# A grouped convolution with per-patch experts on one core: ScalarE's turn in another order, with the window write on its queue

## The reference, cut to what matters

```
x: (32 images, 32 channels, 32, 32), float32
v = (x - mean) / sqrt(var + 1e-5)          # over each channel's 32x32 (group norm, one channel a group)
v is padded to 40x40; patches of 8x8 with a border of 1: 5x5 per image, each 10x10, 32 channels
logits = mean of the patch @ Wg + bg        # 8 experts
routing = the largest logit's expert, with its softmax probability
y = relu(conv3x3(patch, Wexp[expert]) + bexp[expert]) * probability
out = x + y                                 # the inner 4x4 patches of each image
```

## Time and profile before

| | |
|---|---|
| time, median of 3 runs (lowest to highest) | 201.89 us (200.23 to 203.51) |
| the profiled execution: time, span | 200.15 us, 198.0 us |
| granted clock of TensorE, mean over the span | 0.829 |
| busy: PE, DVE, ACT, POOL | 107.9, 116.4, 92.9, 75.9 us |
| DMA queue 1, queue 10 | 48.8%, 28.3% of 16 engines' span |

### The profile page before, as it was taken

The page is one execution under the profiler, slowest core; times in us unless marked ns, Lnnn a source line. Parts: engine busy times, 40 slices in busy tenths (PEclk is TensorE's granted clock), DMA queues, the critical chain, the costliest instruction groups (busy, mean ns, idle before and its releaser), DMA issues.

```text
span 198.0 us, 11471 instructions
## 1 busy us (share of the span) xinstructions
PE 107.9 (54%) x4894; PEld 102.5 (52%) x4894; DVE 116.4 (59%) x270; ACT 92.9 (47%) x253; POOL 75.9 (38%) x236
## 2 busy tenths in 40 slices
PE   0004136738395709970593719960692749808930
PEld 0003135728395709960592718960692749708930
DVE  3796923625199706992199705992199309691264
ACT  2586375920693337550693237650693262513200
POOL 0850673733202671054702562043803562538000
PEclk9999999696969685698599675698599678966997
DMA  5974899776869975899559975899559956898302
GB/s 186 480 325 165 183 279 359 296 188 230 219 240 313 335 262 203 323 282 362 187 214 320 336 247 203 309 286 359 211 216 309 318 187 269 228 322 308 119 0 106
DMA packets 41553, 50.93 MB, mean 257 GB/s; under 512 B 31136, under 2 KB 33312, under 8 KB 40480
## 3 DMA queue, kind: packets, MB, share of 16 engines
q1 hardware_dynamic: 33088, 29.18, 48.8%
q10 hardware_dynamic: 8448, 21.56, 28.3%
HBM read 17.32 MB, written 14.43 MB: 160 GB/s over the span
## 4 chain that ended last, share of the span: by engine, by line
ACTq 21%; DMA 20%; DVE 16%; ACT 13%; PE 12%; SPq 8%; issue 8%; DVEq 0%
ACTq L120 13%; DMA XG<-windows 12%; PE conv_bank L507 10%; SPq L171 8%; DMA XG<-XG 6%; ACTq L437 6%; ACT WS L427 5%; ACT WIND L416 5%; DVE BLK L329 3%; DMA XT<-x 2%; ACT XN L405 2%; DVE BLK L333 2%; DVE XT L337 1%; DVE STATS L257 1%; PE pick_bank L495 1%
## 5 line engine op out<-in xcount | busy, mean ns | idle before, releaser
L507 PE MATMUL conv_bank<-XG,WS 128*32 128x64 f32 x4800 | 95.9, 253 | 42.4 <-DMA XG<-XG 35.3
L507 PEld LDWEIGHTS conv_bank<-XG,WS 128*32 128x32 f32 x4800 | 90.7, 132 | 44.6 <-DMA XG<-XG 36.9
L214 POOL COPY WS<-WP 128x192 f32 x200 | 61.9, 357 | 101.0 <-issue 64.8
L427 ACT COPY WS<-WP 128x192 f32 x200 | 54.5, 348 | 76.2 <-issue 60.2
L322 DVE STREAM_TRANSPOSE YT<-conv_bank 128x320 f32<-128x320 f32 x40 | 18.8, 493 | 18.1 <-PE conv_bank L507 18.1
L264 DVE TENSOR_SCALAR NEWT<-ROOT,VAR 128x1 f32<-128x1 f32 x8 | 2.2, 272 | 41.5 <-ACT ROOT L397 41.5
L489 PE MATMUL logit_bank<-GATE,CONST 128*100 128x8 f32 x40 | 6.1, 261 | 33.1 <-DVE GATE L287 33.1
L489 PEld LDWEIGHTS logit_bank<-GATE,CONST 128*100 128x100 f32 x40 | 5.2, 199 | 34.5 <-DVE GATE L287 18.6
L416 ACT COPY WIND<-XN 128x2500 f32<-128x2500 f32 x8 | 19.0, 2376 | 0.2
L329 DVE STREAM_TRANSPOSE BLK<-YT 128x1024 f32<-128x1024 f32 x8 | 17.9, 2231 | 1.1
L405 ACT ACTIVATE XN<-XT,NEGMR,RSTD 128x1024 f32<-128x1024 f32 x8 | 10.2, 1274 | 8.5 <-DVE NEGMR L269 8.5
(11 more groups left out here) (36 smaller groups left out, 45.9 us busy)
## 6 DMA issues: line engine op xcount, KB each, us to landing
XG<-XG ACTq DMA_DIRECT2D x30, 490.0 KB, 4.1
windows<-WIND SPq DMA_DIRECT2D x8, 1250.0 KB, 5.6
XG<-windows SPq DMA_DIRECT2D x60, 125.0 KB, 4.2
XT<-x SPq DMA_DIRECT2D x8, 512.0 KB, 6.6
out<-XT SPq DMA_DIRECT2D x16, 256.0 KB, 4.2
XG<-XG ACTq DMA_DIRECT2D x16, 240.0 KB, 2.4
XG<-windows SPq DMA_DIRECT2D x32, 62.5 KB
XG<-ones ACTq DMA_DIRECT2D x1, 1250.0 KB, 11.1
```

What stands on the lines that cost most here:

```text
L214: last = nc.gpsimd.tensor_copy(WS[:, at % RING, ACT_PAIRS + i, :], WP[:, bass.ds(index[i], PAIR)])
L427: last = nc.scalar.copy(WS[:, at % RING, i, :], WP[:, bass.ds(index[i], PAIR)])
L507: last = nc.tensor.matmul(o, WS[:, lot, n % LOT * 2 + b // 2, column:column + C], taps, start=kx == 0, stop=kx == TAPS - 1)
```

## The change

- `windows_dram` has three buffers instead of two (`WB`).
- `write_windows` moves from SyncE's list to ScalarE's, behind `windows`, for every group; ScalarE waits for the copy into WIND before it asks. `shift` is the same code at another place, called with the engine.
- ScalarE's turn begins with `copies(g,4)`, then `exponent(g+1)`, `shift(g,2)`, `normalise(g+2)`, `windows(g+2)`, `write_windows(g+2)`, then as before; `root(g+3)` stands at the turn's end instead of `root(g+2)` at its start, and `root(2)` ahead of the loop.
- VectorE: `statistics(g+3)` between lots 1 and 2 instead of `statistics(g+2)` at the turn's start; `finish` is split into `weigh` (transpose, relu and probability) and `add`, with `selection(g+1)` between them; `gate(g+2)` after lot 0's transpose instead of lot 1's.

```diff
--- before.py
+++ after.py
@@ -20,6 +20,7 @@
 LOT, LOTS = NB, NP // NB
 NCB = LOTS
 XB = 5
+WB = 3
 SQ = 32
 HALF = H * W // 2
 SEG = 2
@@ -88,7 +89,7 @@
         conv_bank = [bank(f"conv_bank{i}") for i in range(NCB)]
         logit_bank, pick_bank = bank("logit_bank"), bank("pick_bank")
 
-        windows_dram = [nc.dram_tensor(f"windows{u}", (GI * C * NP, WIN * WIN), fp32).ap() for u in range(2)]
+        windows_dram = [nc.dram_tensor(f"windows{u}", (GI * C * NP, WIN * WIN), fp32).ap() for u in range(WB)]
 
         x_loaded = [sem(f"x_loaded{i}") for i in range(XB)]
         table_loaded, small_loaded, ones_loaded = sem("table_loaded"), sem("small_loaded"), sem("ones_loaded")
@@ -131,6 +132,15 @@
                     engine.dma_start(rows, source[:, 0:PART[1] * LOT, ky * WIN:ky * WIN + TAP]
                                      ).then_inc(lower_loaded[0] if tail else first_loaded, 16)
 
+        def shift(engine, g, part):
+            first, last = PART[part] * LOT, PART[part + 1] * LOT
+            size = (last - first) * PATCH - (TAPS - 1) * WIN
+            engine.wait_ge(upper_loaded[part], UPPERS * (g if part == 0 else g + 1))
+            for ky in range(1, TAPS):
+                rows = bass.AP(XG, ky * KEPT + first * PATCH, [[ROWS * KEPT, C], [NP * PATCH, GI], [1, size]])
+                source = bass.AP(XG, first * PATCH + ky * WIN, [[ROWS * KEPT, C], [NP * PATCH, GI], [1, size]])
+                engine.dma_start(rows, source).then_inc(lower_loaded[part], 16)
+
         def lay_even(e):
             return (bass.AP(WP, e * E * PAIR, [[E * E * PAIR, KP], [PAIR, E], [1, NW]]),
                     bass.AP(BLK, e * NW, [[H * W, KP], [0, E], [1, NW]]))
@@ -147,19 +157,6 @@
             def load_x(g):
                 sp.dma_start(XT[g % XB][:], x_rows[g]).then_inc(x_loaded[g % XB], 16)
 
-            def write_windows(g):
-                sp.wait_ge(windows_ready, g + 1)
-                if g > 1:
-                    for part in range(1, SPLITS):
-                        sp.wait_ge(upper_loaded[part], UPPERS * (g - 1))
-                    if g > 2:
-                        sp.wait_ge(upper_loaded[0], UPPERS * (g - 2))
-                    else:
-                        sp.wait_ge(first_loaded, FIRSTS)
-                        sp.wait_ge(lower_loaded[0], LOWERS)
-                sp.dma_start(windows_dram[g % 2].rearrange("(p k) w -> p (k w)", k=NP), WIND[:]
-                             ).then_inc(windows_written, 16)
-
             def read_upper(g, part):
                 first, last = PART[part] * LOT, PART[part + 1] * LOT
                 sp.wait_ge(windows_written, 16 * (g + 1))
@@ -167,7 +164,7 @@
                     sp.wait_ge(conv_done, LOTS * (g - 1) + PART[part + 1])
                 for b in range(GI):
                     rows = bass.AP(XG, (b * NP + first) * PATCH, [[ROWS * KEPT, C], [PATCH, last - first], [1, PATCH]])
-                    source = windows_dram[g % 2].rearrange("(b n j) w -> b j n w", b=GI, j=C)[b]
+                    source = windows_dram[g % WB].rearrange("(b n j) w -> b j n w", b=GI, j=C)[b]
                     sp.dma_start(rows, source[:, first:last]).then_inc(upper_loaded[part], 16)
 
             def stores(g):
@@ -180,14 +177,10 @@
             load_x(1)
             load_x(2)
             load_x(3)
-            write_windows(0)
             read_first(sp, range(TAPS - 1))
             read_upper(0, 1)
             read_upper(0, 2)
-            write_windows(1)
             for g in range(GROUPS):
-                if g + 2 < GROUPS:
-                    write_windows(g + 2)
                 if g > 0 and g + 3 < GROUPS:
                     if g + 3 >= XB:
                         sp.wait_ge(out_stored, 32 * (g + 3 - XB + 1))
@@ -322,7 +315,7 @@
                 nc.vector.transpose(to, conv_bank[at % NCB][:, 0:LOT * PIX].rearrange("p (n s q) -> p n s q", s=2, q=SQ)
                                     ).then_inc(bank_free[lot], 1)
 
-            def finish(g):
+            def weigh(g):
                 for lot in range(LOTS):
                     dve.wait_ge(bank_free[lot], g + 2)
                 blocks = bass.AP(YT, 0, [[2 * NP * C, 128], [NB, KEEP], [1, KEEP], [NP * C, 2], [NP, C]])
@@ -331,6 +324,8 @@
                 patches = BLK[:].rearrange("p (k w) -> p k w", w=PIX)
                 prob = bass.AP(PBM[g % 3], 0, [[SPREAD, 128], [1, SPREAD], [0, PIX]])
                 then_next(nc.vector.scalar_tensor_tensor(patches, patches, 0.0, prob, ALU.max, ALU.mult))
+
+            def add(g):
                 for v in range(KEEP):
                     rows = XT[g % XB][:, v * PS * W:(v + 1) * PS * W].rearrange("p (i h w) -> p h i w", i=PS, h=KEEP)
                     strip = BLK[:, v * PS * W:(v + 1) * PS * W].rearrange("p (h i w) -> p h i w", i=PS, h=KEEP)
@@ -359,10 +354,9 @@
             probability(0)
             selection(0)
             gate(1)
+            statistics(2)
 
             for g in range(GROUPS):
-                if g + 2 < GROUPS:
-                    statistics(g + 2)
                 if g + 1 < GROUPS:
                     routing(g + 1)
                 if g + 2 < GROUPS:
@@ -373,19 +367,24 @@
                     nc.vector.memset(SPARE[:, LOTS:LOTS + 1], 0.0).then_inc(pick_ready, 1)
                 if g > 0:
                     turn_lot(g - 1, LOTS - 1)
-                    finish(g - 1)
+                    weigh(g - 1)
                 if g + 1 < GROUPS:
                     selection(g + 1)
+                if g > 0:
+                    add(g - 1)
                 turn_lot(g, 0)
-                turn_lot(g, 1)
                 if g + 2 < GROUPS:
                     gate(g + 2)
                 else:
                     nc.vector.memset(SPARE[:, LOTS + GROUPS - g:LOTS + GROUPS - g + 1], 0.0).then_inc(gate_ready, 1)
+                turn_lot(g, 1)
+                if g + 3 < GROUPS:
+                    statistics(g + 3)
                 turn_lot(g, 2)
                 turn_lot(g, 3)
             turn_lot(GROUPS - 1, LOTS - 1)
-            finish(GROUPS - 1)
+            weigh(GROUPS - 1)
+            add(GROUPS - 1)
 
 
         @block.scalar
@@ -427,14 +426,18 @@
                     last = nc.scalar.copy(WS[:, at % RING, i, :], WP[:, bass.ds(index[i], PAIR)])
                 last.then_inc(act_copied[lot], 1)
 
-            def shift(g, part):
-                first, last = PART[part] * LOT, PART[part + 1] * LOT
-                size = (last - first) * PATCH - (TAPS - 1) * WIN
-                act.wait_ge(upper_loaded[part], UPPERS * (g if part == 0 else g + 1))
-                for ky in range(1, TAPS):
-                    rows = bass.AP(XG, ky * KEPT + first * PATCH, [[ROWS * KEPT, C], [NP * PATCH, GI], [1, size]])
-                    source = bass.AP(XG, first * PATCH + ky * WIN, [[ROWS * KEPT, C], [NP * PATCH, GI], [1, size]])
-                    act.dma_start(rows, source).then_inc(lower_loaded[part], 16)
+            def write_windows(g):
+                act.wait_ge(windows_ready, g + 1)
+                if g >= WB:
+                    for part in range(1, SPLITS):
+                        act.wait_ge(upper_loaded[part], UPPERS * (g - WB + 1))
+                    if g > WB:
+                        act.wait_ge(upper_loaded[0], UPPERS * (g - WB))
+                    else:
+                        act.wait_ge(first_loaded, FIRSTS)
+                        act.wait_ge(lower_loaded[0], LOWERS)
+                act.dma_start(windows_dram[g % WB].rearrange("(p k) w -> p (k w)", k=NP), WIND[:]
+                              ).then_inc(windows_written, 16)
 
             act.dma_start(WT, wtab).then_inc(table_loaded, 16)
             act.dma_start(CONST[:], consts).then_inc(small_loaded, 16)
@@ -448,6 +451,7 @@
             act.wait_ge(pads_set, 1)
             normalise(0)
             windows(0)
+            write_windows(0)
             for e in ACT_LAYS[2:]:
                 last = nc.scalar.copy(*lay_odd(e))
             last.then_inc(pairs_laid, 1)
@@ -455,31 +459,34 @@
             normalise(1)
             exponent(0)
             windows(1)
+            write_windows(1)
             act.wait_ge(pairs_laid, 3)
             act.wait_ge(index_ready, 1)
             copies(0, 0)
             read_first(act, [TAPS - 1])
             for lot in range(1, LOTS - 1):
                 copies(0, lot)
-            shift(0, 1)
+            shift(act, 0, 1)
+            root(2)
             for g in range(GROUPS):
-                if g + 2 < GROUPS:
-                    root(g + 2)
+                copies(g, LOTS - 1)
                 if g + 1 < GROUPS:
                     exponent(g + 1)
+                shift(act, g, 2)
                 if g + 2 < GROUPS:
                     normalise(g + 2)
                     windows(g + 2)
-                shift(g, 2)
-                copies(g, LOTS - 1)
+                    write_windows(g + 2)
                 if g + 1 < GROUPS:
                     act.wait_ge(index_ready, g + 2)
```

(8 more changed lines are left out.)

## The result

The changed kernel takes 216.43 us (215.35 to 217.03, 4 runs) against 201.48 in the same comparison: ratio 1.076, 95% interval 1.068 to 1.083, slower. The forecast was 212.0, with 200 to 220 around it. Medians are over all executions of a kernel, ratios and their intervals over the faster ones alone, those within 1.5% of its fastest. The profiled execution took 216.41 us, its span is 214.6 against 198.0: 16.6 us to account for.

What follows compares the result with a forecast made beforehand. Bound taken: a ring of ScalarE's turn through WIND and the DMA queue. Four turns 4.2, last turn with a write 2.5, turn without one 2.2 and start 3.0 add 11.9 to 200.15: 212.0 us, range 200 to 220.

Steps and rivals of the forecast that it cites:

- The ring through ScalarE, WIND and the queue: Pace of the kernel before: ScalarE's turn to WIND, 13.32 us, then 9.1 us of SyncE's DMA queue until part 0's reads land.
- Lot 4's copies make normalise 2.9 us later: ScalarE's turn: index load 1.9, copies 1.4, exponent 0.3 and requests 0.3 put normalise at 79.8 instead of 76.87.
- The sum for a full turn: A turn with window write and x load gets 1.05 us longer: 2.96 later, 1.9 quicker.
- Root ran ahead of the turn: ScalarE: deviation is long done when normalise comes, so the 1.03 us from root to normalise goes.
- The write's alternation with the reads: DMA queues: 1.4 small read packets pass per large write packet, about 180 of 1280, gaining the reads 0.3 us.
- That the reads cannot be ahead, and the write sets their landing: Part 0's reads, first requested at 82.5 to 84.2, stay behind the write's packets from 84.4; landing 90.7 against 89.66.
- TensorE isn't in it: Kernel before: part 0's first read request, after TensorE's convolutions, went at 82.09 while the queue was busy to 87.
- The turn without a write: The turn from 155.05 to 172.57: paced by exponent, index and copies; exponent 3.6 us later, index 1.43 sooner, +2.2 us.
- The start: Until the first part's request at 45.06: early write delays the root 1.6 us; request at 48.1, +3.0, bounds 0 and 4.8.
- The rest at nothing: Three DRAM buffers, selection before the adds, statistics within the turn and the earlier gate were costed at nothing.
- the load comes back at once: Rival, 13%: the index load before lot 4's copies takes 0.54 us and part 2's requests hide wholly; 200.6 us, no change.
- The reads get ahead of the write: Rival, 11%: lot 1 ends two or three microseconds before the write is asked for, ScalarE alone sets the pace; 193 us.

## Why the prediction was right, step by step

- **The ring through ScalarE, WIND and the queue: right, and shown** by the run with lot 4's copies early and the exponent ahead of them: 8.98 us from the write's request to the tap copies', and a turn of 24.9.
- **Lot 4's copies make normalise 2.9 us later: right in kind, 2.4 us by the trace.** It starts 12.0 us after the turn's first request, where it was 9.6. 2.95 from the root's end to normalise against 1.03 is 1.9, and the root itself stands 0.4 later in the turn; the write is asked for 15.7 us after the turn's first request, where it was 13.35. The forecast was 16.3: the load took 1.2 and not 1.9 in this turn, 1.6 in the middle ones. The sum for a full turn was 1.05; the middle ones took 1.2, in part by luck, as the point on the reads says.
- **"Root ran ahead of the turn": wrong in its reason.** The root at the end of a turn is the instruction right ahead of the next turn's first, so it isn't earlier at all. Its round trip through VectorE is hidden only because lot 4's copies now stand between it and normalise; in the version with these put back, normalise waits 0.83 us for VectorE again. The 1.03 was taken off rightly.
- **The write's alternation with the reads: right in kind.** 109 small packets beside 135 large ones in 3.9 us, 0.8 for each large one, with the reads asked for as it began; 1.4 was assumed. The Trainium skill's page "DMA: Bandwidth & Descriptors", section "Queues, rings and completion order", has the engines go round robin between queues by packets of typically 9 to 17 descriptors; these rows fit a grain of about one large row against one small instead.
- **That the reads cannot be ahead, and the write sets their landing: the step that was half the truth.** The times were right (lot 1's end and the write's packets within half a microsecond of each other, as the two ways in the text had it), but I took the exponent's way for a reason why the reads come late, and not as a ring of its own. It is one, of 11.4 us to the exponent and 11.9 from there to the next request, and where there is a write it was the longer by about a microsecond: that much a turn lost when the exponent came early. In all the time fell by 12 us then, more than my theory could give. The middle turns of that run are 0.5 us longer than before, and what sets them is the way through WIND; so that the changed kernel's came out at 1.2 beside a forecast of 1.05 is luck, since the ring that was summed is not the one that set them. The text also said "TensorE isn't in it" of the kernel before. The ring through tap copies, lot 0 and lot 1 reached SyncE's reads there at 82.02, and alone these need 5.3 us to the request (94.65 to 99.93 in the run with the late exponent): 20.1 against the turn's 22.4, so the statement held, by 2.3 us.
- **The turn without a write: mis-sized by 2.5 of 4.73 us, by that same omission.** I took exponent, index and copies for its ring. The exponent came 3.1 us later in the turn (11.1 against 8.0), for 3.6 forecast. But then the reads bind, as the chain shows:

```profile
178.74 0.10 ACT LEXP L409
...
180.38 3.26 PE conv_bank L514 x115
...
185.66 4.00 DMA XG<-windows
```

Lot 1 ran at a granted clock of 0.50, the lower level of 1.2 GHz, after lot 0 at 0.50 and a stand for the picks from 176.8 to 179.1; before, TensorE went from lot 0 (0.54) to the picks without a stand, and lot 1 ran at 1.00, the upper level of 2.4 GHz. The windows view, the changed kernel's row and the one of the kernel before:

```profile
179.90:183.60 3.70, 3.70 (x138) 3.69 (x141) 3.63 (x5) 0.00 (x0) 0.00 (x0) 0.50 0.10 40
```

```profile
164.80:166.80 2.00, 2.00 (x136) 1.99 (x139) 1.97 (x2) 0.13 (x1) 0.00 (x0) 1.00 0.96 375
```

The difference, 1.7 us, would be the greater part of the 2.5, an estimate from these two rows. In the run with the exponent one place earlier TensorE didn't stand there either, the clock from 172 to 176 was 1.00, and the turn took 16.34.

- **The start: right, in its two terms too.** The early write made the first convolution 2.6 us later and the root 1.1 (it began at 32.57 to 32.71 in four traces with the write on ScalarE's queue, at 31.45 to 31.49 in three with it on SyncE's), where 1.6 was taken; the new order added 1.3 to 1.7, where the sum had 1.4.
- **The first turn, +3.20 for +1.05: not foreseen.** Part 1's tap copies came 8.07 us into the turn, as they waited for late reads, against 6.95 before, and the load behind them took 2.70 us. That the x load, now freed from the write and asked for at 55.99, moved its packets in front of these copies' fits the trace; no run separated it. With group 1's write asked for later these copies came 7.25 us into the turn, and it took 24.4.
- **The rest at nothing: right**, 0.997 for all of it, the overlooked move of the logits included. The parts weren't run one by one.
- Of the rivals, "the load comes back at once" named the right lever, since the load ahead of the bulk gave 8.4 us back; but in the changed kernel it stood behind the bulk in every turn. "The reads get ahead of the write" is what the run with the exponent one place earlier shows; it paid less than the rival's 193, since the load behind the write then took 4.36 us and not the 0.55 to 1.2 that the rival wanted.

## What to carry to other kernels

Before moving work in an engine's list, follow every result that the displaced instructions make, and time each ring that closes through them from its own start to the next turn's; a ring with 3 us of slack doesn't show in the chain of waits and is next when the move is 3 us long. Two rings that both pass the point of the move have to be relieved together, and a run that relieves one tells only the distance to the other. When a change bundles a cheap gain with a dear reordering, cut it in four corners: here the queue was worth 2% in the old order and the order cost 9 to 10. A factor that measures little in these corners can be worth much between them: the queue gave some 12 us where only the exponent was put early.

## What the runs showed of the hardware

A register load from IDX in SBUF took 0.54 us at the least and up to 4.45 us behind bulk transfers that read SBUF, on ScalarE and on GpSimd alike; these are all loads of the changed kernel, with 4.87 us in the run with the write behind the tap copies:

```profile
L121 POOLq TENSOR_LOAD <-IDX x40: 557/1180/4451, 19.9 to 194.2; - x40
L121 ACTq TENSOR_LOAD <-IDX x40: 542/1582/4433, 20.8 to 198.4; - x40
```

Moved ahead of the bulk, the load for lot 4 took 0.54 instead of 1.20; the load for lot 2, moved behind another bulk, took 4.33. The Trainium skill's page "DMA: Bandwidth & Descriptors", section "Latency and other measured facts", gives about 600 ns as a floor for such a load; the shortest here, 0.54, are a little under it. What mattered here is how far above it the loads rose.
